# Row search: the layout of the pair numbers that TensorE reads as its moving operand

## The reference

```python
logits = x @ gate_W
probs = jax.nn.softmax(logits.astype(jnp.float32), axis=-1)
rw, sel = jax.lax.top_k(probs, TOP_K)
rw = rw / rw.sum(axis=-1, keepdims=True)
w_full = jnp.sum(jax.nn.one_hot(sel, NUM_EXPERTS, dtype=rw.dtype) * rw[..., None], axis=1)
...
expert_out = jnp.concatenate([mlp_out, kan_out], axis=0)
out = jnp.einsum('eth,te->th', expert_out, w_full)
```

## Time and profile before

| | before |
|---|---|
| median of 3 runs | 728.19 us (725.35 to 728.44) |
| profiled execution | 732.84 us |
| its span | 731.0 us |
| TensorE matmuls, busy | 577.0 us (79%) |
| TensorE weight loads, busy | 470.5 us (64%) |
| VectorE, busy | 455.7 us (62%) |
| ScalarE, busy | 274.2 us (38%) |
| GpSimd, busy | 251.5 us (34%) |

### The profile page before, as it was taken

The page is one execution under the profiler, slowest core; times in us unless marked ns, Lnnn a source line. Parts: engine busy times, 40 slices in busy tenths (PEclk is TensorE's granted clock), DMA queues, the critical chain, the costliest instruction groups (busy, mean ns, idle before and its releaser), DMA issues. The chain is left out here.

```text
span 731.0 us, 18200 instructions
## 1 busy us (share of the span) xinstructions
PE 577.0 (79%) x6003; PEld 470.5 (64%) x6004; DVE 455.7 (62%) x1172; ACT 274.2 (38%) x766; POOL 251.5 (34%) x314
## 2 busy tenths in 40 slices
PE   5349979999998458776999859743999899999870
PEld 5236668888887424654788735542666688888870
DVE  5644447887887498798133474655444577887744
ACT  2222234554554116601556413141323445554420
POOL 6037752443343245700000030111677433433320
PEclk9999998999999869777899979955899999999985
DMA  8973330000000120000000000199111000000005
GB/s 268 346 279 88 92 96 22 14 22 14 14 15 17 44 84 3 3 13 4 12 5 4 3 0 1 36 342 367 66 50 50 23 15 14 18 18 14 14 12 176
DMA packets 41679, 48.94 MB, mean 67 GB/s; under 512 B 7328, under 2 KB 33280, under 8 KB 40352
## 3 DMA queue, kind: packets, MB, share of 16 engines
q1 hardware_dynamic: 32480, 36.08, 15.0%
q0 software_dynamic: 4928, 10.10, 5.0%
q10 hardware_dynamic: 4224, 2.10, 1.0%
HBM read 38.05 MB, written 10.22 MB: 66 GB/s over the span
## 5 line engine op out<-in xcount | busy, mean ns | idle before, releaser
L981 ACT ACTIVATE k_sig<-k_h1T 128x256 f32<-128x256 f32 x264 | 84.5, 402 | 144.7 <-DVE k_h1T L872 144.7
L774 PEld LDWEIGHTS k_y_ps<-kan_w,k_basis 128*128 128x128 f32 x1056 | 127.3, 198 | 7.2 <-issue 5.6
L774 PE MATMUL k_y_ps<-kan_w,k_basis 128*128 x1056 | 127.8, 281 | 5.1 <-DVE k_basis L847 5.1
L764 PE MATMUL k_z_ps<-kan_w,k_basis 128*128 x528 | 126.3, 394 | 0.0
L764 PEld LDWEIGHTS k_z_ps<-kan_w,k_basis 128*128 128x128 f32 x528 | 100.6, 195 | 16.9 <-issue 0.8
L847 DVE SCALAR_TENSOR_TENSOR k_basis<-k_sig 128x512 f32<-128x512 f32 x132 | 85.6, 690 | 10.6 <-ACT k_sig L981 10.6
L640 POOL DMA_INDIRECT y_rows<-k_y,k_rows_out x33 | 42.2, 1280 | 106.2 <-DVE k_y L879 100.3
L974 ACT ACTIVATE k_sig<-k_h0T 128x128 f32<-128x128 f32 x264 | 55.8, 294 | 3.3 <-DVE k_h0T L835 3.3
L898 DVE TENSOR_TENSOR m_z<-m_z_ps,mlp_b 128x512 f32<-128x512 f32 x40 | 27.7, 692 | 42.8 <-PE m_z_ps L743 42.8
L1457 DVE TENSOR_REDUCE p_minus_max<-p_ps 128x6 f32<-128x960 f32 (+1 forms) x44 | 46.0, 1118 | 6.8 <-PE p_ps L1374 5.3
L1493 ACT ACTIVATE got<-p_ps 128x960 f32<-128x960 f32 (+1 forms) x44 | 39.2, 944 | 27.5 <-PE p_ps L1409 27.5
(11 more groups left out here) (228 smaller groups left out, 913.2 us busy)
## 6 DMA issues: line engine op xcount, KB each, us to landing
kan_w<-in_L_ffn_kan_sl_W_dram SPq DMA_DIRECT2D x16, 1024.0 KB, 11.1
x_rows<-got SPq DMA_DIRECT2D x4, 1024.0 KB, 13.2
mlp_w<-in_L_ffn_mlp_W_dram SPq DMA_DIRECT2D x2, 1024.0 KB, 6.1
mlp_w<-in_L_ffn_mlp_W_dram SPq DMA_DIRECT2D x8, 256.0 KB, 7.3
mlp_b<-in_L_ffn_mlp_b_dram SPq DMA_DIRECT2D x2, 1024.0 KB, 8.4
got<-y_rows SPq DMA_DIRECT2D x8, 256.0 KB, 4.8
got<-y_rows ACTq DMA_DIRECT2D x8, 256.0 KB, 5.4
xs<-in_L_attn_x_dram SPq DMA_DIRECT2D x4, 256.0 KB, 3.6
```

Of the source, the lines that this page charges most:

```text
L764: last = nc.tensor.matmul(z_ps, basis0[:, g], k.kan_w0[:, bass.ds(e, 1), g], start=(g == 0), stop=(g == G - 1))
L774: last = nc.tensor.matmul(y_ps, basis1[:, g, c], k.kan_w1[:, bass.ds(e, 1), c, g], start=(g == 0 and c == 0), stop=(g == G - 1 and c == F2 ...
L981: ins = nc.scalar.activation(sig1[:, g], h1T[:], ACT.Sigmoid, bias=float(-GRID[g]))
```

## The change

`numbers` is laid out with the pairs outermost: `[P, 2, NS, TOPK * NT]` becomes `[P, TOPK * NT, 2, NS]`. The two writers address it through a rearranged view, in the order of `in_slot` as before, and TensorE reads one contiguous stretch of 92 numbers for each pair. `in_slot` and `in_row` keep their layouts. No instruction and no wait is added or removed.

```diff
@@ -245,7 +245,7 @@
         in_slot = sb("in_slot", [P, NS, TOPK * NT], F16)
-        numbers = sb("numbers", [P, 2, NS, TOPK * NT], F16)
+        numbers = sb("numbers", [P, TOPK * NT, 2, NS], F16)
@@ -368,7 +368,7 @@
-                nc.vector.tensor_tensor(numbers[:, 0], in_slot[:], bc(k.pair_no[:], 1, NS),
+                nc.vector.tensor_tensor(numbers[:, :, 0].rearrange("p v s -> p s v"), in_slot[:], bc(k.pair_no[:], 1, NS),
                                         ALU.mult).then_inc(numbers_ready, 1)
@@ -497,7 +497,7 @@
-                        last = nc.tensor.matmul(found_ps[:], in_row[:, :, v], numbers[:, :, :, v], start=(v == 0),
+                        last = nc.tensor.matmul(found_ps[:], in_row[:, :, v], numbers[:, v], start=(v == 0),
                                                 stop=(v == TOPK * NT - 1))
@@ -512,7 +512,7 @@
-                nc.scalar.activation(numbers[:, 1], in_slot[:], ACT.Copy, scale=k.one_up[:]).then_inc(numbers_ready, 1)
+                nc.scalar.activation(numbers[:, :, 1].rearrange("p v s -> p s v"), in_slot[:], ACT.Copy, scale=k.one_up[:]).then_inc(numbers_ready, 1)
```

## The result

The change made the kernel slower: median 733.99 us of 11 runs (731.07 to 739.59) against 728.19 of 11 (724.79 to 732.74), ratio 1.0087 with a 95% interval of 1.0057 to 1.0117. The forecast was no change, 728.2 us, in a range of 725.0 to 730.0. The profiled execution took 735.53 us, its span 733.7 us.

A forecast was written before the change was run, and what follows sets the result against it. No single engine was taken to bound the kernel; the first gather waits for the landing of `x_rows`. The search's +0.76 - 1.95 = -1.2 us each is hidden, gain 0 in both blocks: 728.2 us, range 725.0 to 730.0.

The forecast's parts named there:

- The gate, and the hiding: First gather in both blocks: waits for the landing of `x_rows`, so a search 1.2 us shorter gains 0.
- The reading of L462 against the name in the waits: GpSimd's first gather: waits for both `x_rows` writes and `rows_ready` at 1, not for L393, which the timeline names.
- Part 1: TensorE's search matmuls: contiguous moving operand cuts the step from 170 to 107 ns, 1.95 us less a search.
- Discounting the rule: TensorE's stationary operand: despite the 16-byte line rule, its stride costs next to nothing, by loads of 148 against 142 ns.
- Part 2: VectorE's product (L371): stepped writes fall to one element a cycle, 1689 ns, +0.76 us a search.
- the row that I called nearest: VectorE scan writing 16 numbers 32 bytes apart, 180 ns against 175 adjacent; taken to show stepped writes don't stall.
- Part 3: ScalarE's scaled copy (L515): stays near 1523 ns with stepped writes, 1.45 us of cover, costs nothing.
- The doubling that I allowed for: ScalarE's copy (L515): were its time to double, it would end at 33.1 and cost 0.1 us.
- C: Both writers: stepped 2-byte writes stall, product 5.2 us or more, 4.1 us lost in all, 732.3 us; chance 0.03.
- A: TensorE's part not shortened, only VectorE's +0.76 us left, search longer; price 0.6 to 1.1 us, 729.0 us; chance 0.12.
- B: The search gates most executions, so its 1.2 us counts in each block: -2.4 us, 725.8 us; chance 0.07.

The follow-up runs named there:

- row_order: Changed kernel with the two writers' loops turned, so writes of `numbers` are adjacent and reads of `in_slot` step by 64 bytes; ratio 1.0013 to the kernel before.
- quad: Kernel before with `numbers` laid out in groups of four pairs, the write of `x_rows` not moved; ratio 0.998 (0.9952 to 1.0009).
- probe: Kernel before plus scratch writes in several patterns by VectorE and ScalarE, alone and together; 184-byte step alone 7.216 and 7.347 us.
- probe_sizes: Kernel before plus scratch work on VectorE and TensorE at steps of 2 to 64 bytes; VectorE's first write, at 16 bytes, took 6.78 us.
- serial: Changed kernel with ScalarE's copy (L515) started only when VectorE's product (L371) is done; 744.35 us in one run.

## Why the prediction was wrong, point by point

**The gate, and the hiding.** Right, with the margin read from rows 3 to 5. Two searches shorter by 1.2 us (row_order) and 2.6 us (quad) gained nothing. A longer one was paid past the margin. By the forecast's own reckoning the search came 3.22 us later, less about 0.2 and 0.5 us, so 5.7 us for the two; the medians differ by 5.80 us. That match is closer than the traces bear out: 4.0 us of it arrive at TensorE's first product, just below the 4.2 to 8.5 us of the interval. Where the rest comes from, if it is more than scatter, stays open. The reading of L462 against the name in the waits held too: as soon as the landing came clearly last, the wait was put down to it. But the margin isn't fixed, as the two probes show, which run the code of before and add theirs behind its last block. There L437 landed at 38.6 and 37.0 us in block one instead of 39.65, and the gather started 0.98 us after the search (L391) in both: the search was the gate. It was so in block two of probe as well, while in block two of probe_sizes the landing came last.

**Part 1, TensorE.** The direction was right and the size too small: 2.98 us a search instead of 1.95. I let the weight load set the new step, at 107 ns. The step fell to (2.64 - 0.28)/31 = 76 ns, so the pair of load and matmul doesn't need 107 ns. What holds it at 76 ns isn't shown. It would be 92 columns at 1.2 GHz, but the first search took the same time at a granted clock of 1.00 as the second at 0.50, and the loads were busy for nearly all of it (window, its length, PE and PEld busy, granted clock, DMA share, GB/s):

```profile
38.40:41.20 2.80, 2.64 (x32) 2.48 (x32) 1.00 0.79 315
503.40:506.20 2.80, 2.65 (x32) 2.49 (x32) 0.50 0.96 385
```

The Trainium skill's rule of 16-byte lines (Advanced Engine Details and Errata, Memory Cachelines) held for the moving operand in probe_sizes, but for a tenth: one use of each line 157 to 165 ns a matmul, two uses 84, adjacent numbers 75. It didn't show for the stationary one, which stepped by 64 bytes in the changed kernel and took part in steps of 76 ns. Discounting the rule there was right.

**Part 2, VectorE's product: the step that failed.** I took +0.76 us, one element a cycle, and it was +6.28. The 0.76 was the right price for the lost rate, as the adjacent fp32 write of probe_sizes shows (1.69 us, as forecast). What was put at nothing is the step itself, about 1.03 us (2.72 for fp32 at 184 bytes), and the stall of a 2-byte write on top, about 4.5 us. The error lies in the row that I called nearest. The scan of rows 8 writes fp32 numbers, and 16 of them; its extra was read as "no stall". But a write of 16 fp32 numbers 32 bytes apart could at most show 16 x 0.7 = 11 ns, about what its 180 against 175 ns leaves room for, and it says nothing of 2-byte numbers. The honest bound was the sentence that no row shows a stepped 16-bit write, and an unknown cost of an instruction of 1472 elements needed more than 3 in 100. That instruction is first on a chain with 0.2 us of margin. The Trainium skill's rule of lines (Advanced Engine Details and Errata, Memory Cachelines), which I weighed for TensorE's reads, I didn't put to the writers. It gives a penalty but no size, and it would have warned of the 1.03 us, not of the larger part, which belongs to the narrow write.

**Part 3, ScalarE's copy.** It cost nothing only because VectorE's product took as long: it ended at 37.41, and TensorE waited for `in_row` until 38.47. The doubling that I allowed for was nearly a fivefold time. The two instructions of L375 took 2.59 instead of 2.35 us, but that isn't ScalarE's doing: in serial, where it wrote on until 44.65, they took 2.59 us too. Their record begins 0.41 us before the end of L371, where it was 0.08.

**The rivals.** C was the mechanism: stepped 2-byte writes stall the writers. It was priced at 5.2 us for the product, and the total of 4.1 us more came from that; with 6.28 us more and TensorE's 2.98 less its own sum gives 5.9. Its chance of 0.03 was the fault. A didn't happen. B's condition, the search as the gate, was met in some executions of the old code (the probes, above), but B's gain wasn't: the search grew instead, and row_order, whose search is the 1.2 us shorter that B priced, gained nothing measurable.

## What to carry to other kernels

A layout change moves a stride from one side to the other; price the side that gets it by rows with the same number width and length, and where there is none, take the unknown as the widest term of the sum. If reader and writer want different orders, a layout in short groups (here four 2-byte numbers, 8 bytes) gave the writers their full rate and cost the reader little (3.03 us against 2.64). And before shortening a search, look at what else its consumer waits for: here the layout paid only together with the earlier write of `x_rows`.

## What the runs showed of the hardware that was not expected

Per number, with the fixed 158 ns taken off and 1472 numbers: an fp16 write at 184 bytes 4.8 ns on VectorE; at 16 bytes 4.5 ns; at 8 bytes 2.3 ns; at 4 bytes 1.12 ns; in runs of two 0.90 ns and of four 0.52 ns, the same as adjacent. An fp32 write costs 1.04 ns adjacent or at 8 bytes and 1.76 at 16; an fp16 read at 16 bytes 1.76 and at 8 bytes 1.04. So at steps of 16 bytes or more there are two costs: about 0.7 ns a number for the step, for reads and writes alike, and 2.7 to 3.1 ns more if a write is only 2 bytes wide. Neither is shared out evenly at smaller steps: at 8 bytes the first is gone and the second 1.2 ns, at 4 bytes hardly 0.1. ScalarE pays nearly the same (7.35 us against 1.52), and two engines that do it at once don't slow each other (7.215 and 7.347 us together, 7.216 and 7.347 alone). What in the memory makes the narrow write slow was not taken apart.
